# A four-stage graph and expert kernel: two expert layers computed from split operands, and a reordered round, head and end

## What is computed

```
x = x + L0_gnn(layernorm(x), adj)      # attention over neighbours, softmax, ELU
x = x + L0_ffn(layernorm(x))           # 6 experts, the best 2 weigh in
x = x + L1_gnn(layernorm(x), adj)
x = x + L1_ffn(layernorm(x))           # 8 experts of 256 wide, 2 per graph, GELU, layer norm

# L0_ffn, dense over all experts e:
h1 = relu(x @ w1[e] + b1[e]); h2 = relu(h1 @ w2[e] + b2[e])
out = sum_e weight[e] * (h2 @ w3[e] + b3[e])
# L1_ffn, the router works on the mean of a graph:
logits = mean(x) @ Wr + br; rw = softmax(logits); rw = softmax(rw * scale(rw))
top_w, top_i = top_k(rw, 2); top_w = softmax(top_w)
```

## Time and profile before

| what | value |
|---|---|
| median of 3 runs | 597.38 us (595.43 to 598.31) |
| the profiled execution | 596.36 us, its span 594.6 us |
| PE busy | 554.5 us, 93% |
| DVE busy | 452.0 us, 76% |
| ACT busy | 413.3 us, 70% |
| POOL busy | 232.9 us, 39% |
| full rounds | 106.46 to 380.69 us |
| head | about 452 to 468 us |
| tail and end | 468 to 594.6 us |

### The profile page before, as it was taken

The page is one execution under the profiler, slowest core; times in us unless marked ns, Lnnn a source line. Parts: engine busy times, 40 slices in busy tenths (PEclk is TensorE's granted clock), DMA queues, the critical chain, the costliest instruction groups (busy, mean ns, idle before and its releaser), DMA issues.

```text
span 594.6 us, 15169 instructions
## 1 busy us (share of the span) xinstructions
PE 554.5 (93%) x3858; PEld 459.2 (77%) x3859; DVE 452.0 (76%) x1653; ACT 413.3 (70%) x1101; POOL 232.9 (39%) x449
## 2 busy tenths in 40 slices
PE   7679999999899999999999999999868899999993
PEld 5456678777677777777787787777657799999992
DVE  3767978889798888889889898776555277777777
ACT  1346666878678687786887878867733478888883
POOL 6212214442333434334243342331332036666664
PEclk9989999999999999999999999999998699999997
DMA  8505314143150522505235052032020377877732
GB/s 208 109 5 156 107 54 162 31 132 111 52 160 1 159 72 88 157 3 160 66 93 160 1 159 95 13 108 89 19 71 2 119 221 240 246 220 217 225 110 71
DMA packets 78833, 66.45 MB, mean 112 GB/s; under 512 B 9916, under 2 KB 64460, under 8 KB 78796
## 3 DMA queue, kind: packets, MB, share of 16 engines
q1 hardware_dynamic: 65562, 60.60, 33.9%
q10 hardware_dynamic: 13234, 5.42, 3.4%
HBM read 61.57 MB, written 4.42 MB: 111 GB/s over the span
## 4 chain that ended last, share of the span: by engine, by line
PE 54%; DVE 13%; issue 10%; DMA 9%; POOL 4%; ACT 4%; SPq 3%; ACTq 1%; DVEq 1%; POOLq 0%
DMA x<-in_x 8%; PE bank L1481 8%; PE bank L1468 7%; PE bank L1698 5%; PE wide L1698 4%; PE bank L1708 4%; PE wide L1708 4%; PE wide L239 3%; PE wide L206 3%; SPq L628 3%; PE bank L1460 2%; PE bank L1461 2%; PE bank L1462 2%; DMA w_scratch<-wrow 2%; DVE at_stats L87 1%
## 5 line engine op out<-in xcount | busy, mean ns | idle before, releaser
L1481 PE MATMUL bank<-w,h2w 128*128 128x128 f32 x768 | 103.4, 278 | 1.1 <-DVE h2w L1062 1.1
L1468 PE MATMUL bank<-h,w 128*128 128x512 f32 x192 | 99.0, 597 | 0.5 <-ACT h L816 0.3
L1481 PEld LDWEIGHTS bank<-w,h2w 128*128 128x128 f32 x768 | 94.9, 192 | 4.6 <-DVE h2w L1062 2.0
L811 ACT ACTIVATE h<-bank,b 128x512 f32<-128x512 f32 x96 | 66.3, 691 | 42.5 <-PE bank L1468 42.5
L816 ACT ACTIVATE h<-bank,b 128x512 f32<-128x512 f32 x96 | 66.0, 687 | 12.8 <-PE bank L1462 12.5
L1062 DVE TENSOR_TENSOR h2w<-h,wide_w 128x512 f32<-128x512 f32 x96 | 64.7, 676 | 9.4 <-ACT h L811 9.3
L1460 PE MATMUL bank<-xnTh,w1h 128*128 128x512 f32 x96 | 67.1, 699 | 0.0
L100 POOL TENSOR_TENSOR route_var_eps<-route_mean_var,eps 128x4 f32<-128x4 f32 x16 | 10.5, 654 | 103.5 <-DVE route_mean_var L93 103.4
L100 POOL TENSOR_TENSOR at_var_eps<-at_mean_var,eps 128x4 f32<-128x4 f32 x32 | 12.4, 386 | 98.5 <-DVE at_mean_var L93 98.5
L268 ACT ACTIVATE at_pr<-at_lk,at_nm 128x128 f32<-128x128 f32 x128 | 41.2, 413 | 3.4 <-DVE at_nm L303 3.4
L239 PE MATMUL wide<-at_wh,at_prT 128*128 128x129 f32 x256 | 34.5, 278 | 3.7 <-ACT at_prT L275 3.7
(11 more groups left out here) (264 smaller groups left out, 1397.0 us busy)
## 6 DMA issues: line engine op xcount, KB each, us to landing
wide_w<-w_scratch SPq DMA_DIRECT2D x96, 256.0 KB, 4.4
mask<-in_L_ffn_W SPq DMA_DIRECT2D x124, 128.0 KB, 2.5
x<-in_x SPq DMA_DIRECT2D x16, 256.0 KB, 5.7
adj_in<-in_adj SPq DMA_DIRECT2D x16, 256.0 KB, 6.3
wide_w<-bmix_scratch SPq DMA_DIRECT2D x16, 256.0 KB, 3.6
xin<-in_x SPq DMA_DIRECT2D x15, 256.0 KB, 6.0
out<-at_pr ACTq DMA_DIRECT2D x8, 256.0 KB, 3.0
out<-at_prT ACTq DMA_DIRECT2D x7, 256.0 KB, 2.9
```

The costliest lines, as they stand in the source:

```text
L811: a.activation(h2[:, e % 2, :], b_h2[:, :], ACT.Relu, bias=b2[:, e:e + 1]).then_inc(h2_ready, 1)
L1468: pe.matmul(b_h2[:, :], w2[:, e, :], h1[:, e % 2, :], start=True, stop=True).then_inc(l2_done, 1)
L1481: last = pe.matmul(b_out[:, s], h2w[:, e % 2, s], w3[:, e, :], start=False, stop=(e == E0 - 1), skip_group_check=True)
```

## The change

It has four parts.

**Split products.** For experts 3 and 5 (`SPLIT`) `layer2` becomes three float32r products. `relu1` runs twice for them on ScalarE, once into `h1h` (rounded to float32r) and once into `h1` as before; GpSimd forms `h1l = h1 - h1h` (`low`); VectorE splits the weights once (`split_w2`). The third product waits for `h1l_ready`.

**Order of the round.** `layer1` of expert 3 stands before `layer2` of expert 2, and that of 5 before `layer2` of 4, on TensorE and ScalarE. ScalarE's `pe0` stands behind `relu1` of expert 4. SyncE issues the loads of the next group ahead of the last two `wide_w` transfers.

**Head.** The experts are chosen from the products before their exponential, 24 filling products on TensorE become 3 and 8 smaller ones, the tail's first `up` waits for `gidx` but no longer for the gates and the bias mix, whose products stand behind the second and third `up`. GpSimd waits for `gidx` before its first sum. ScalarE's GELU table is loaded behind the copies of the first weights.

**End.** The group before the last is finished and stored ahead of the last group.

```diff
+SPLIT = {3: 0, 5: 1}
...
+        with eng.Fori(3, end, 2) as i:
...
+            def weights(g, par, ahead):
...
                 for e in range(E0):
-                    if e > 0:
-                        settle(sp, const_ready)
-                        need(sp, h2w_ready, (g - 1) * E0 + e + 1)
+                    if e == 4:
+                        ahead()
+                    settle(sp, const_ready)
+                    need(sp, h2w_ready, (g - 1) * E0 + e + 1)
                     sp.dma_start(wide_w[:, e, :], w_dram[par, e].partition_broadcast(P)).then_inc(w_loaded[e], 16)
...
+                def ahead():
+                    if i0 >= 1 - LEAD["norm0"] and live("norm0", i0, 1):
+                        load(i + 4, i0 % 2)
+
                 if live("route", i0):
-                    weights(i + 1, (i0 + 1) % 2)
-
-            rounds(sp, body)
+                    weights(i + 1, (i0 + 1) % 2, ahead)
+                else:
+                    ahead()
+
+            rounds(sp, body, N - 6)
...
             sp.wait_ge(gidx_ready, 1)
             load_w1(0, 0, 2, 2)
+            load_w1(1, 1, 0, 3)
             sp.wait_ge(bmix_step, E1 + 3)
             sp.dma_start(bmix_dram[:, :], bmix[:, :]).then_inc(bmix_stored, 16)
-            load_w1(1, 1, 0, 2)
+            load_w1(1, 1, 3, 1)
             sp.wait_ge(bmix_stored, 16)
             load_bmix(0, 0)
-            load_w1(1, 1, 2, 2)
             load_bmix(1, 1)
...
+                def low(e):
+                    n = i * E0 + e
+                    p.wait_ge(h1_ready, n + 1)
+                    need(p, l2_done, n - 1)
+                    p.tensor_tensor(h1l[:, :], h1[:, e % 2, :], h1h[:, :].bitcast(F32), ALU.subtract)\
+                        .then_inc(h1l_ready, 1)
...
+                if live("experts", i0):
+                    low(3)
                 if live("attn1", i0) and i0 != N:
                     attn_pool_split(at1, p, zero, i - 1)
...
+                if live("experts", i0):
+                    low(5)
                 if live("route", i0, 1) and i0 != -LEAD["route"]:
                     norm_root(rn, p, eps, minus_half, i + 2, rn["xn_ready"])
...
+            p.wait_ge(gidx_ready, 1)
...
+            finish(N - 2, 0)
             norm_root(fn, p, eps, minus_half, N - 1, fn["xn_ready"])
-            finish(N - 2, 0)
...
                 a.wait_ge(l1_done, n + 1)
+                if e in SPLIT:
+                    need(a, l2_done, n - 1)
+                    a.activation(h1h[:, :], b_h1[:, :], ACT.Relu, bias=b1[:, e:e + 1])
                 a.activation(h1[:, e % 2, :], b_h1[:, :], ACT.Relu, bias=b1[:, e:e + 1]).then_inc(h1_ready, 1)
...
                 if run:
                     relu1(n + 3, 3)
+                    relu2(n + 2, 2)
                 if i0 == 0:
                     route_relu(1)
                 if attn0:
...
-                if route:
+                def route_exp():
                     a.wait_ge(route_step, ROUTE * (i + 1) + 2)
                     a.activation(pe0[:, :, :], lgd[:, :, :], ACT.Exp).then_inc(pe0_ready, 1)
-                if run:
-                    relu2(n + 3, 3)
+
...
                 if attn0:
                     attn_act_prT(at0, a, i + 2)
                 if run:
+                    relu2(n + 3, 3)
                     relu1(n + 4, 4)
+                if route and i0 != -LEAD["route"]:
+                    route_exp()
...
-                if run:
-                    relu2(n + 4, 4)
...
+                if run:
+                    relu1(n + 5, 5)
                 if attn0:
                     attn_act_elu(at0, a, i + 2)
                 if run:
-                    relu1(n + 5, 5)
+                    relu2(n + 4, 4)
...
-            a.wait_ge(head_dve, 9)
-            a.activation(hd[:, 8, :], hd[:, 6, :], ACT.Exp, bias=hd[:, 2, 0:1]).then_inc(head_act, 1)
-            a.wait_ge(head_dve, 15)
+            a.wait_ge(head_dve, 7)
+            a.activation(hd[:, 8, :], hd[:, 6, :], ACT.Exp).then_inc(head_act, 1)
+            a.wait_ge(head_dve, 8)
+            a.activation(hd[:, 9, :], top8[:, :], ACT.Exp).then_inc(head_act, 1)
+            a.wait_ge(head_dve, 13)
             a.activation(hd[:, 11, 0:2], hd[:, 10, 0:2], ACT.Exp).then_inc(head_act, 1)
...
             norm_apply_act(fn, a, buf_tile(sm[0]), buf_tile(sm[0]), N - 2)
+            store(N - 2, 0)
             for q in range(2):
-                a.wait_ge(fin_ready, N - 1 + q)
+                a.wait_ge(fin_ready, N + q)
                 a.dma_start(outg[N - 1][:, 2 * q:2 * q + 2, :], tiles(fin[1][:, :])[:, 2 * q:2 * q + 2, :])\
                     .then_inc(stored[1], 16)
-            a.wait_ge(fin_ready, N + 1)
-            a.dma_start(outg[N - 2], tiles(fin[0][:, :])).then_inc(stored[0], 16)
             a.wait_ge(stored[0], 8 * N)
...
+            def split_w2():
+
+                for e, q in SPLIT.items():
+                    v.tensor_copy(w2h[:, q, :], w2[:, e, :]).then_inc(split_step, 1)
+                v.wait_ge(split_step, 14)
+                for e, q in SPLIT.items():
+                    v.tensor_tensor(w2l[:, q, :], w2[:, e, :], w2h[:, q, :].bitcast(F32), ALU.subtract)\
                         .then_inc(split_step, 1)
...
+                if i0 == -LEAD["route"]:
+                    split_w2()
...
             step(v.reciprocal(h(5), b_misc[0:NG, 0:E1]))
-            step(v.tensor_scalar(h(5), h(5), CAPACITY / P, 1.0, ALU.mult, ALU.min))
-            step(v.tensor_tensor(h(6), h(4), h(5), ALU.mult))
-            minus_max(h(6), 2)
+            step(v.scalar_tensor_tensor(h(6), h(5), P / CAPACITY, h(1), ALU.min, ALU.mult))
+            step(v.max(top8[:, :], h(6)))
+            step(v.max_index(top8i[:, :], top8[:, :], h(6)))
+            v.tensor_copy(pairs[:, 2:4], top8i[:, 0:2]).then_inc(head_diag, 1)
             v.wait_ge(head_act, 2)
-            step(v.max(top8[:, :], h(8)))
-            step(v.max_index(top8i[:, :], top8[:, :], h(8)))
-            v.tensor_copy(pairs[:, 2:4], top8i[:, 0:2]).then_inc(head_diag, 1)
             step(v.tensor_reduce(h(2, 1), h(8), AX, ALU.add))
             step(v.reciprocal(h(2, 1), h(2, 1)))
-            step(v.tensor_scalar(h(9, 2), top8[:, 0:2], h(2, 1), None, ALU.mult))
+            v.wait_ge(head_act, 3)
+            step(v.tensor_scalar(h(9, 2), h(9, 2), h(2, 1), None, ALU.mult))
+            step(v.tensor_scalar(h(10, 2), h(9, 2), h(9, 1), None, ALU.subtract))
...
+            finish(N - 2, 0)
...
+                if e in SPLIT:
+                    pe.wait_ge(h1_ready, n)
...
+            def layer2(n, e, g):
+                if e in SPLIT:
+                    pe.wait_ge(h1_ready, n + 1)
+                    need(pe, h2_ready, n)
+                    pe.matmul(b_h2[:, :], w2h[:, SPLIT[e], :], h1h[:, :], start=True, stop=False)
+                    pe.matmul(b_h2[:, :], w2l[:, SPLIT[e], :], h1h[:, :], start=False, stop=False)
+                    pe.wait_ge(h1l_ready, 2 * g + SPLIT[e] + 1)
+                    pe.matmul(b_h2[:, :], w2h[:, SPLIT[e], :], h1l[:, :], start=False, stop=True)\
+                        .then_inc(l2_done, 1)
+                    return
...
-                    layer2(n + 2, 2)
                     layer1(n + 3, i, par, 3)
+                    layer2(n + 2, 2, i)
...
-                    layer2(n + 4, 4)
                     layer1(n + 5, i, par, 5)
+                    layer2(n + 4, 4, i)
...
-            for j in range(24):
-                pe.matmul(b_h1[:, 0:P], w1h[:, (j % E0) * P:(j % E0 + 1) * P], xnTh[:, 0, 0:P], start=True, stop=True,
-                          skip_group_check=True)
+            busy(b_h1, 3)
             pe.wait_ge(head_diag, 1)
             for k in range(2):
                 last_t = pe.matmul(b_misc[0:1, k * NG:(k + 1) * NG], pairs[:, 2 + k:3 + k], ident[0:NG, 0:NG],
                                    start=True, stop=True, skip_group_check=True)
             last_t.then_inc(head_pe, 1)
-            busy(b_h1, 6)
...
+            busy(b_h1, 8)
+            pe.wait_ge(xnT3_ready, N)
             pe.wait_ge(gidx_ready, 1)
...
+                    if t == 1 and g0 == 0:
+                        gates_rows()
                     if t == 2:
                         need(pe, sum_ready, g - 1)
                     if t == 2 and g0 == 0:
+                        bias_rows()
+                    if t == 2 and g0 == 1:
                         pe.wait_ge(gw_ready, 1)
+                        pe.wait_ge(bmix_step, E1 + 3)
                     if t >= 2:
                         down(GG * g + t - 2, gpar, t - 2, pairs_of[t - 2 + early])
```

More of the change, by code:

```diff
@@ L403, in build @@
     w3 = sb("w3", [P, E0, P])
+    w2h = sb("w2h", [P, 2, P], F32R)
+    w2l = sb("w2l", [P, 2, P], F32R)
+    h1h = sb("h1h", [P, GW], F32R)
+    h1l = sb("h1l", [P, GW], F32R)
     b1 = sb("b1", [P, E0])
@@ L506, in build @@
     h1_ready = sem("h1_ready")
+    h1l_ready = sem("h1l_ready")
     h2_ready = sem("h2_ready")
@@ L540, in build, with rounds @@
     LATE = 16 * 9
```

(41 more changed lines are left out.)

43 lines of the change are left out of this document (24 added, 19 removed).

## The result

The changed kernel takes 603.01 us (median, 602.58 to 606.1), beside 596.4 us for the kernel before in the same runs: a ratio of 1.0123, with a 95% interval from 1.0079 to 1.0167. It is 1.2% slower; 588 us and "faster" were wrong. The profiled execution took 606.1 us, its span is 604.3, so 9.7 us above that of before.

What follows compares the result with a forecast made beforehand. Rounds were taken as bound by TensorE's work, after the change by ScalarE's loop. Full rounds -1.5, others -1.0, head -5.9, end -0.9 gave -9.3 us, so 588 us; own range 585 to 591, 8 in 10 579.5 to 592.5.

Steps and rivals of the forecast that it cites:

- The products: Split `layer2` on TensorE: three float32r products take about 0.70 us instead of 0.86, saving 0.16 a layer, 0.32 a round.
- ScalarE's loop: Full rounds: ScalarE's order closes a loop through `at1_pr` in 24.79 us, so eleven rounds give -1.5 us.
- costs nothing here: ScalarE's stretch before `at1_pr`: `relu2(4)`, the ELU and `relu1(5)` change places at no cost.
- GpSimd against VectorE: Rounds: a GpSimd subtraction over 128x512 can hold VectorE for 0.9 us, making `weigh(2)` some 0.8 us later.
- I add nothing: Stall of 0.6 us before `layer3(4)`, said to lie where TensorE would wait for `at1_pr` anyway; priced at nothing.
- The blocked VectorE that "adds up": Rival: holds of 0.8 and 1.3 us reach `weigh(4)`, `wgt` and the router's root; rounds 25.1, kernel 591.5 us; chance 0.14.
- TensorE stays the limit: Rival: `pq` and the pooled norm are not late; rounds take 24.12 us, the kernel 580 us; chance 0.23.
- The slower rival: Expert 5's subtraction is late and shifts `layer2(5)` to `at1_pr`, 1.2 us a round; kernel 601 us; chance 0.05.
- The other rounds: The five rounds with fewer stages save at most 0.32 us each: -1.0 us, from 0 to -1.6.
- the excess: Eleven full rounds: time over TensorE's own work, 5.4 us, tied to late loads of `x`; not all to come back.
- Head and end: Head -5.9 us (-3.6 to -7.9) by an earlier first `up`; end -0.9 us (0 to -1.9) by a smaller last store.
- The range: Range for 8 in 10 for the kernel's time: 579.5 to 592.5 us.

Runs made afterwards that it cites:

- c_relu2_first: The changed kernel with `relu2` of expert 4 moved ahead of the ELU of `at0` on ScalarE: 606.4 us, ratio 1.0170 to before, 25.77 us a round.
- a_nosplit: The changed kernel without the split products, its new order, loads, head and end kept: 585.9 us, ratio 0.9811 to before, 24.55 us a round.
- g_onerelu: The changed kernel with one ReLU for experts 3 and 5, GpSimd subtracting `h1h` from itself: 590.0 us, ratio 0.9911 to before, 24.54 us a round.
- f_nolow: The changed kernel without GpSimd's subtractions, the third product reading `h1h`: 592.3 us, ratio 0.9935 to before, 24.81 us a round.
- i_dve_low: The changed kernel with the two subtractions on VectorE instead of GpSimd: 593.4 us, ratio 0.9949 to before, 24.88 us a round.
- k_only5: The changed kernel with only expert 5 split: 600.8 us, ratio 1.0083 to before, 25.43 us a round.
- d_old_order: The changed kernel with the order of before on TensorE and ScalarE, split kept: 610.4 us, ratio 1.0237 to before, 25.81 us a round.
- e_headendloads: The kernel before with only the new head, end and order of loads, no split: 583.3 us, ratio 0.9776 to before, 24.40 us a round.

## Why the prediction was wrong

**The products.** I took 0.16 us saved for each split layer, 0.32 a round. The 0.86 us of a float32 `layer2` was right, but the three products for it do not take 0.70: in c_relu2_first they take 388.21 - 387.44 = 0.77 us, the first of them 0.31 until the next starts. With the `layer1` behind it, a float32 `layer2(3)` takes 373.96 - 372.39 = 1.57 us in a_nosplit, three products take 388.92 - 387.44 = 1.48 in c_relu2_first. For expert 5 it is 1.59 and 1.46. Over the full rounds from 130 to 375 us the means are 1.55 and 1.58 in a_nosplit, 1.48 and 1.47 in g_onerelu. So some 0.2 us a round are saved. The rounds show less: 24.49 us in g_onerelu behind its first, 24.55 in a_nosplit.

**ScalarE's loop.** That it sets the round once nothing else is late was right, and so was its length: 24.79 forecast, 24.81 in f_nolow. It closes at another place, `layer2(5)` behind `relu2(4)`, not at `at1_pr`, so that the two numbers agree to 0.02 us is luck. The sentence that the exchange of `relu2(4)`, the ELU and `relu1(5)` "costs nothing here" overlooked that TensorE would wait for `relu2(4)`.

**GpSimd against VectorE: this step failed.** I had the hold (0.8 us on `weigh(2)`) and did not follow it. It was priced for `weigh(4)`, found to lie beside the loop, and then "I add nothing". What it delays is VectorE's queue behind it: `at1_wh`, the mask and the statistics of the pooled norm, and with these that norm's root on GpSimd and `p_xn` on ScalarE. `weigh(2)` takes 0.70 us longer, ScalarE's wait is 0.72, and 24.81 + 0.72 = 25.53 us, the measured round. Taking the subtraction out (f_nolow, 24.81) or off GpSimd (i_dve_low, 24.88) takes that wait away, but for one of 0.4 us in i_dve_low. The work of a shared resource was charged to the instruction it hits, not to the chain that runs through it. The hold has no fixed size: 0.70 us on `weigh(2)`, 1.05 in k_only5 (1.74 instead of 0.69), so 0.9 was no upper bound. What stayed the same is the end. The subtraction ends at 307.29 and `weigh(2)` at 307.84, 0.55 behind; in d_old_order it is 347.47 and 348.02, in k_only5 340.43 and 340.98, in g_onerelu 298.43 and 298.97. It is 0.55 us for all 18 products `h2w` of the changed kernel that began during a subtraction, 15 `at_lk` of d_old_order and 10 `at_prT` of k_only5. So VectorE does nearly all of its own work, 0.55 of 0.68 us, after GpSimd is done, whatever was left of that. By the Trainium skill (SBUF — State Buffer, "Who interferes with whom") the two exclude each other for the whole instruction; the traces agree in these four places.

**The rivals.** The blocked VectorE that "adds up" (25.1 us, 0.14) was the right mechanism with the wrong path and too small a size. "TensorE stays the limit" is what a_nosplit and e_headendloads do, both without the split. The slower rival named the subtraction for expert 5; TensorE never waited for it in the full rounds (it does in d_old_order, 0.9 us a round). The measured 25.53 lies just under its point of 25.64, and the kernel was slower all the same, because of the next step.

**The other rounds: -1.0 forecast, +8.6 measured** up to the root. Three more waits of about 1 us before `layer2(5)` are in it, and TensorE waits 2.2 us for `at_src`, whose split stands behind the subtraction on GpSimd, where it waited 0.9 before. From the last `at_wh` to the root it is 15.9 us instead of 14.8: the granted clock fell to 0.50, the 1.2 GHz level, from 461 to 464 us, behind three microseconds (457 to 460) in which TensorE was busy for 1.1. In the kernel before and in a_nosplit, which have the same wait of 1.9 us for `at_pr`, it stayed at 1.00 up to the root; why is open. In a_nosplit the whole stretch is 73.7 us, in e_headendloads 72.0, without the subtractions (f_nolow) 77.0 and with them on VectorE (i_dve_low) 75.3. So most of the 8.6 us come with the split, and 4 to 5 of them with its subtractions on GpSimd; I did not settle every part of it.

**Loads, head, end.** VectorE's wait for `x` went from 10.4 to 0.8 us, and e_headendloads shows its worth: 5.8 us, where the excess was put at 5.4. The changed kernel can't use it. Head and end: -5.6 to -6.6 in the traces with them, forecast -6.8. Counted with the head of before the first `up` stands at 461.7, forecast 461.5.

**The sum.** Full rounds +6.6 instead of -1.5, the others +8.6 instead of -1.0, head and end -5.6 instead of -6.8, the start +0.2: 9.7 against -9.3. The range reached to 592.5 only, because I had not followed the hold of `weigh(2)` to the root of the pooled norm.

## What to carry to other kernels

When an engine that shares something with another gets new work, look up what the other does in those microseconds, and follow the delay through every queue behind it to the next wait of the bottleneck; an engine at 39% of its time can still lie in the loop that sets the round. Price a saving on the busiest engine in the place where it stands, with its neighbours: 0.32 us hoped for were 0.2 in the products, while splitting one expert in the old order cost 0.4 us a round, and the two ReLUs in the new one 0.26. And time the parts of a compound change apart: head, end and loads alone give 583.3 us, 2.2% below the kernel before, and the split and the order take 20 us back.
